# A tile loop whose output rows are normed and stored one tile earlier, with GpSimd's stores in front of its root

## The chip, the cores and the metric

The kernel runs on one core of a Trainium2 chip, as one launch. Every time here is device time of that core in microseconds (us). The kernel before was timed in three runs; one further execution was recorded by the hardware profiler, and all durations below are from that execution. The engines are TensorE (PE, with its weight loads as PEld), VectorE (DVE), ScalarE (ACT), GpSimd (POOL) and SyncE (SP, which here only starts DMA transfers).

## The reference, cut to what matters

The layer has three parts in a row, each followed by a residual sum and a layer norm. The first two are a selective state-space scan and a slot attention with three rounds of a gated cell. The change touches the third alone, a routed feed-forward layer with 8 experts over 64 x 128 tokens of 128 features:

```
x = x.reshape(-1, 128)                       # 8192 tokens
route = sigmoid(x @ Wr + br)
max_prob, max_ind = max(route), argmax(route)
for e in range(8):
    y = gelu(x @ W1[e]) @ W2[e]              # 128 -> 512 -> 128
    out += (max_ind == e) * y
out = out * max_prob
x = layernorm(x + out)                       # (v - mean) / sqrt(var + 1e-5) per token
```

## The kernel before, in words

The program has three stages, each a block of its own. The second leaves the tokens in a DRAM buffer, `sorted_x`, sorted by expert, with each token's probability and number beside it. The third stage, `expert_stage`, walks over that buffer in 39 tiles of 256 rows (`NJ`), each padded to belong to a single expert. It is the stage that the change touches.

Each engine has its own program, written out by hand as `tile(j, buf, turn, half)`, and `over_tiles` (L1470) unrolls it: tiles 0 to 8 one by one, then 30 tiles in a hardware loop of 6 at a time with `j` in a register, then a tail of a few tiles in which the late steps are finished. In its tile `j` an engine does steps that belong to tile `j` and to earlier tiles; `within(j, n)` asks whether tile `j - n` exists. Buffers are rings of six (`NBUF`), so `buf` is `j % 6`, and an even `buf` is an even `j`. The steps are these; "k" is the tile that a step works on.

- PE: in its tile j the transposes of tile j (L1657), the up matmuls of tile j-1 (L1668) and the down matmuls of tile j-2 (L1677). The down matmuls of tile k wait until `total` of tile k-2 has been written (`need(pe, summed, j - 1)`), since the two share a PSUM bank.
- ACT: in its tile j the two Gelus of tile j (L1560), and then the norm of tile j-5 (L1550): two activations, one for each half of 128 rows, that write `orow` from `total`, `shift` and `rstd`. For an even k it first waits until `shift` of the pair (k, k+1) is there; for each it waits until the store of tile k-6 has landed.
- DVE: in its tile j the copy of the transposed rows (L1607); in an odd tile j then `shift` of the pair that begins at j-5 (L1612), which waits for POOL's root; then for tile j-3 the target rows (L1617), `total` (L1619), and the moments (L1625, L1629); in an even tile j last `veps` of the pair that begins at j-4 (L1635).
- POOL: in an even tile j the root of the pair that begins at j-4 (L1526: `rstd` = `veps` to the power -0.5, for both tiles of the pair in one instruction, after a wait for `veps`); then the store of tile j-6 (L1531): a wait for the norm of that tile, and two indirect DMAs that scatter 128 rows each to `out_x`.
- SP: loads the rows and the two weight matrices of tile j, once `total` of tile j-6 has been written.

All of an engine's instructions run in the order in which they stand. POOL's root for a pair is therefore behind every store that is written before it, and DVE's `shift`, and with it all that follows on DVE, is behind the root.

Of the kernel before, what the change touches and what calls it, by code (L numbers as in the profile page):

```python
# [29 lines left out]
def need(eng, sem, value):  # L30

    if isinstance(value, int) and value <= 0:
        return
    eng.wait_ge(sem, value)


def hold(eng, sem, value, passed):


    eng.wait_ge(sem, value)  # L40
    eng.sem_inc(passed, 1)
# [1359 lines left out]
def expert_stage(nc, t, sb, psum, sem, ident, xs, scattered, base, base_start, e_index, out):  # L1401
# [7 lines left out]
    NJ = (NT + NE * (ROWS - 1)) // ROWS  # L1409
# [25 lines left out]
    ended = sb("ended", [P, NJ, NE])  # L1435
# [34 lines left out]
    def over_tiles(eng, tile, tail):  # L1470

        for j in range(PEEL):
            tile(j, j % NBUF, j // NBUF, j // 2)
        with eng.Fori(0, (NJ - PEEL) // NBUF) as i:
            for k in range(NBUF):
                j = PEEL + k
                tile(i * NBUF + j, j % NBUF, i + j // NBUF, i * (NBUF // 2) + j // 2)
        for j in range(NJ, NJ + tail):
            tile(j, j % NBUF, j // NBUF, j // 2)

    def earlier(buf, turn, back):

        return (buf - back) % NBUF, turn if buf >= back else turn - 1

    def within(j, back):

        return not isinstance(j, int) or back <= j < NJ + back

    def width(j):

        return min(2, NJ - j) if isinstance(j, int) else 2

    @blk.sync
    def _(sp):
        sp.wait_ge(step, N_STEPS)

        def load_rows(j, buf):
            r = sp.value_load(first_row[0:1, bass.ds(j, 1)], min_val=0, max_val=xs.shape[0] - ROWS)
            sp.dma_start(xrow[:, buf], xs[bass.ds(r, ROWS)].rearrange("(s p) d -> p s d", p=P)).then_inc(rows_in[buf], 16)

        def load_weights(j, buf):
            e = sp.value_load(expert[0:1, bass.ds(j, 1)], min_val=0, max_val=NE - 1)
            sp.dma_start(w1[:, buf], t["L0_ffn_W1"][bass.ds(e, 1)].rearrange("e d f -> d (e f)")).then_inc(weights_in[buf], 16)
            sp.dma_start(w2[:, buf], t["L0_ffn_W2"][bass.ds(e, 1)].rearrange("e (c p) d -> p (e c) d", p=P)).then_inc(weights_in[buf], 16)

        def tile(j, buf, turn, half):
            need(sp, summed, j - (NBUF - 1))
            load_rows(j, buf)
            if not isinstance(j, int) or j >= 1:
                load_weights(j, buf)  # L1510
        load_weights(0, 0)
        for lane in range(2):
            sp.wait_ge(scattered[lane], 16 * GB * NQ)
        over_tiles(sp, tile, 0)

    @blk.gpsimd
    def _(pool):
        pool.memset(m_half3[:], -0.5).then_inc(const3, 1)
        pool.memset(all_ones[:], 1.0).then_inc(const3, 1)
        pool.iota(j_index[:], pattern=[[1, NJ]], base=0, channel_multiplier=0, allow_small_or_imprecise_dtypes=True).then_inc(const3, 1)  # L1520
        pool.wait_ge(const3, 3)

        def root(j, buf, pair):
            pool.wait_ge(veps_done, pair + 1)
            w = width(j)
            pool.tensor_tensor(rstd3[:, buf:buf + w], veps3[:, buf:buf + w], m_half3[:, 0:w], ALU.pow).then_inc(rooted3, 1)  # L1526

        def store(j, buf):
            hold(pool, row_done, j + 1, passed3)
            for s in range(HALVES):  # L1530
                pool.indirect_dma_start(out_rows, bass.IndirectOffsetOnAxis(ap=target[:, buf, s:s + 1], axis=0), orow[:, buf, s], None,  # L1531
                                        bounds_check=NT - 1, oob_is_err=False).then_inc(out_stored[buf], 16)

        def tile(j, buf, turn, half):
            if buf % 2 == 0 and within(j, 4):
                root(j - 4, earlier(buf, turn, 4)[0], half - 2)
            if within(j, 6):
                store(j - 6, earlier(buf, turn, 6)[0])
        over_tiles(pool, tile, 6)
        for buf in range(NBUF):  # L1540
            pool.wait_ge(out_stored[buf], 16 * HALVES * len(range(buf, NJ, NBUF)))

    @blk.scalar
    def _(act):
        def normalised(j, buf, turn, pair):
            if buf % 2 == 0:
                act.wait_ge(shifted, pair + 1)
            need(act, out_stored[buf], turn * (16 * HALVES))
            for s in range(HALVES):
                ins = act.activation(orow[:, buf, s], total[:, buf, s], ACT.Identity, bias=shift3[:, buf, s:s + 1], scale=rstd3[:, buf, s:s + 1])  # L1550
            ins.then_inc(row_done, 1)

        def tile(j, buf, turn, half):
            par = buf % 2
            if within(j, 0):
                for m in range(2):
                    act.wait_ge(h_full, j * 2 + m + 1)
                    if m == 0:
                        need(act, y_full, j - 1)
                    act.activation(act_h[:, par, 2 * m:2 * m + 2].rearrange("p c r -> p (c r)"), ps_h[par][m][:], ACT.Gelu).then_inc(h_act, 1)  # L1560
            if within(j, 5):
                last, last_turn = earlier(buf, turn, 5)
                normalised(j - 5, last, last_turn, half - 2)
        over_tiles(act, tile, 5)

    @blk.vector
    def _(dve):
# [151 lines left out]
```

## Time and profile before

| | us |
|---|---|
| median of 3 runs | 1693.28 (1693.16 to 1693.36) |
| profiled execution, its own time | 1696.29 |
| span of its trace | 1694.1 |
| first instruction of `expert_stage` in the trace | 1511.86 |
| first transposes of the tile loop | 1521.44 |
| down matmuls of the last two tiles begin at | 1666.77 |
| last store is issued at | 1684.97 |

Over the whole span PE is busy 87%, DVE 74%, POOL 71% and ACT 65%. Times in the trace are counted from the start of the span. A row of the timeline is one instruction, or several of the same kind one behind the other ("x2"): its start, how long it took, the engine, the line, the operation with what it writes and reads, and in brackets how long the engine had been idle before it and what ended that. The tile to which a row belongs isn't written in it; it is found by counting from the start of the stage. The root at 1656.83 is that of tiles 32 and 33.

### The profile page before, as it was taken

The page shows a single profiled execution, that of the slowest core. Times are in us where ns is not written, and L with a number is a line of the kernel's source. Part 1 is how long each engine was busy: PE and PEld are TensorE (multiplying, and loading weights), DVE is VectorE, ACT ScalarE, POOL GpSimd, SP SyncE. Part 2 cuts the span into 40 slices and gives each one's busy share as a digit, 9 for nine tenths or more (in the row PEclk, how much of TensorE's full clock was granted, in tenths as well). Part 3 has the DMA queues.
Part 4 walks back from the last instruction along what each step waited for, and adds up shares of the span by engine and source line. Part 5 has one row for each costly group of instructions (what it writes and reads, how often), then busy time and mean ns, then how long its engine had stood idle before and what let it go on. Part 6 is the DMA issues. An engine that isn't in the chain of part 4 may idle for free. (4 is left out here: it accounts for less than half of the span.)

```text
span 1694.1 us, 21624 instructions
## 1 busy us (share of the span) xinstructions
PE 1470.6 (87%) x6178; PEld 880.2 (52%) x6178; DVE 1254.2 (74%) x2128; ACT 1099.0 (65%) x2149; POOL 1202.2 (71%) x863
## 2 busy tenths in 40 slices
PE   3888889888898889988885899999999999819994
PEld 1333334333343333433332677777777777619994
DVE  1999999999999999999991367666666666624452
ACT  3777787778877788777863566666566655404553
POOL 1899999999999999999993224555455445543665
PEclk8999999999999999999997999999999999859997
DMA  4454445444455455454431712122032000017771
GB/s 149 138 177 157 157 151 182 161 169 150 163 169 168 158 156 175 157 168 158 153 114 56 276 37 109 54 78 111 15 115 112 14 2 14 13 46 207 214 204 49
DMA packets 105846, 214.17 MB, mean 126 GB/s; under 512 B 12162, under 2 KB 56709, under 8 KB 105744
## 3 DMA queue, kind: packets, MB, share of 16 engines
q1 hardware_dynamic: 101200, 204.50, 36.4%
q0 software_dynamic: 4544, 8.47, 1.5%
q8 instruction: 45, 0.74, 0.2%
q14 instruction: 57, 0.47, 0.1%
HBM read 168.28 MB, written 45.56 MB: 126 GB/s over the span
## 5 line engine op out<-in xcount | busy, mean ns | idle before, releaser
L311 POOL TENSOR_TENSOR hc<-state,c_rows 128x1024 f32<-128x1024 f32 x256 | 598.4, 2359 | 41.4 <-DVE state L479 38.9
L479 DVE TENSOR_TENSOR_SCAN state<-ps_da,inp 128x512 f32<-128x512 f32 x512 | 594.4, 1211 | 25.9 <-ACT ps_da L391 25.9
L568 PE MATMUL ps_y<-hc,ident 128*128 128x512 f32 x1024 | 499.2, 633 | 71.0 <-POOL hc L311 71.0
L391 ACT ACTIVATE ps_da<-dt,a_neg 128x512 f32<-128x512 f32 x512 | 344.7, 687 | 124.3 <-DVE state L479 119.2
L568 PEld LDWEIGHTS ps_y<-hc,ident 128*128 128x128 f32 x1024 | 202.5, 203 | 344.6 <-issue 223.0
L468 DVE TENSOR_TENSOR inp<-dtx,ps_b 128x1024 f32<-128x1024 f32 x192 | 231.4, 1205 | 36.3 <-POOL dtx L286 24.0
L880 POOL TENSOR_TENSOR rs<-ms,m_half 128x4 f32<-128x4 f32 x48 | 49.5, 1032 | 246.1 <-DVE ms L1107 246.0
L298 POOL TENSOR_TENSOR inp<-dtx,b_rows 128x1024 f32<-128x1024 f32 x64 | 150.9, 2358 | 0.0
L521 PE MATMUL ps_misc<-x1T,w_conv 128*128 128x512 f32 (+3 forms) x256 | 119.4, 611 | 30.2 <-ACT x1T L337 22.0
L397 ACT COPY ps_b<-b_rows 128x512 f32<-128x512 f32 x192 | 111.3, 580 | 48.4 <-DVE inp L468 46.6
L1018 ACT ACTIVATE ex<-sc,nmx 77x128 f32<-77x128 f32 x192 | 74.9, 392 | 90.6 <-DVE nmx L1116 90.6
L1531 POOL DMA_INDIRECT out_x<-orow,target x78 | 77.0, 987 | 42.6 <-ACT orow L1550 22.2
L1112 DVE TENSOR_TENSOR sc<-sc,ps_s 77x512 f32<-77x512 f32 x48 | 32.8, 683 | 97.1 <-PE ps_s L1303 97.1
L1560 ACT ACTIVATE act_h<-ps_h 128x512 f32<-128x512 f32 x78 | 46.6, 598 | 82.6 <-PE ps_h L1668 79.5
L521 PEld LDWEIGHTS ps_misc<-x1T,w_conv 128*128 128x128 f32 x256 | 49.1, 197 | 97.1 <-issue 64.5
L919 POOL DMA_INDIRECT sorted_x<-row,dest x64 | 68.0, 1063 | 28.0 <-issue 14.6
L1677 PEld LDWEIGHTS ps_yy<-w,act_h 128*128 128x128 f32 x624 | 75.6, 192 | 2.0
L1668 PE MATMUL ps_h<-xcol,w 128*128 128x256 f32 x312 | 76.0, 388 | 0.0
L1677 PE MATMUL ps_yy<-w,act_h 128*128 128x128 f32 x624 | 75.8, 275 | 0.0
L1315 PEld LDWEIGHTS ps_s<-rse,ex 78*128 78x128 f32 x384 | 48.2, 192 | 33.0 <-DVE rse L1120 25.9
L1607 DVE COPY xcol<-ps_t 128x256 f32<-128x256 f32 x39 | 16.6, 425 | 65.0 <-PE ps_t L1657 65.0
L900 POOL TENSOR_SCALAR row<-tok,mv,rstd 128x128 f32<-128x128 f32 x64 | 58.5, 922 | 5.0 <-POOL rstd L896 5.0
(205 smaller groups left out, 2657.7 us busy)
## 6 DMA issues: line engine op xcount, KB each, us to landing
b_rows<-bc_rows SPq DMA_DIRECT2D x128, 512.0 KB, 4.7
c_rows<-bc_rows SPq DMA_DIRECT2D x128, 512.0 KB, 3.9
sorted_x<-pad_rows SPq DMA_DIRECT2D x8, 4160.0 KB, 14.0
w<-in_L_ffn_W SPq DMA_DIRECT2D x78, 256.0 KB
xrow<-sorted_x SPq DMA_DIRECT2D x39, 130.0 KB
x_tok<-in_x SPq DMA_DIRECT2D x16, 256.0 KB, 3.9
ctx<-in_ctx SPq DMA_DIRECT2D x16, 154.0 KB
out_x<-orow,target POOLq DMA_INDIRECT x78
```

What stands on the lines that cost most here:

```text
L298: pool.tensor_tensor(inp[:, n % RING], dtx[:, par], over_c(b_rows[:, slot, n % 2]), ALU.mult).then_inc(pool_fed, 1)
L311: pool.tensor_tensor(hc[:, n % RING], state[:, n % RING], over_c(c_rows[:, slot, n % 2]), ALU.mult).then_inc(hc_ready, 1)
L391: act.activation(ps_da[u % DA_RING][:], dt[:, par, c], ACT.Exp, scale=a_neg[:, c, n:n + 1]).then_inc(da_ready, 1)
L397: act.copy(ps_b[:], b_rows[:, slot, n % 2]).then_inc(b_copied, 1)
L468: dve.tensor_tensor(inp[:, n % RING], dtx[:, par], over_c(ps_b[:]), ALU.mult).then_inc(dve_fed, 1)
L479: dve.tensor_tensor_scan(state[:, n % RING, c], ps_da[u % DA_RING][:], inp[:, n % RING, c], 0.0, ALU.mult, ALU.add).then_inc(state_ready, 1)
L521: ins = pe.matmul(blocks[:, :, s:], w_conv[:, KW - 1 - s, c * P:(c + 1) * P], x_slot(g).rearrange("p (b l) -> p b l", l=P)[:, :, 0:P - s], ...
L568: ins = pe.matmul(ps_y[:, c], ident[:], hc[:, n % RING, c], start=False, stop=n == NS - 1)
L1018: act.activation(ex[lane][0:M, b * P:(b + 1) * P], sc[lane][:, b * P:(b + 1) * P], ACT.Exp, bias=nmx[lane][:, b:b + 1], accum_out=se[lane] ...
L1531: pool.indirect_dma_start(out_rows, bass.IndirectOffsetOnAxis(ap=target[:, buf, s:s + 1], axis=0), orow[:, buf, s], None, bounds_check=NT ...
L1668: ins = pe.matmul(ps_h[par][m][:, k * ROWS:(k + 1) * ROWS], w1[:, buf, c * P:(c + 1) * P], xcol[:, par], start=True, stop=True)
L1677: ins = pe.matmul(ps_yy[par][:, s * P:(s + 1) * P], act_h[:, par, c, s * P:(s + 1) * P], w2[:, buf, c], start=c == 0, stop=c == FC - 1)
```

## The change

ACT norms tile j-4 in its tile j in place of tile j-5, right behind the Gelus of tile j. POOL stores tile j-5 in its tile j in place of j-6. And in all tiles up to 38 POOL's store now stands in front of the root of its tile; in the tail (`ended`) the root stays in front. The tails of both engines are one tile shorter. DVE, PE and SP are as they were.

```
         def tile(j, buf, turn, half):
-            if buf % 2 == 0 and within(j, 4):
+            ended = isinstance(j, int) and j >= NJ
+            if ended and buf % 2 == 0 and within(j, 4):
                 root(j - 4, earlier(buf, turn, 4)[0], half - 2)
-            if within(j, 6):
-                store(j - 6, earlier(buf, turn, 6)[0])
-        over_tiles(pool, tile, 6)
+            if within(j, 5):
+                store(j - 5, earlier(buf, turn, 5)[0])
+            if not ended and buf % 2 == 0 and within(j, 4):
+                root(j - 4, earlier(buf, turn, 4)[0], half - 2)
+        over_tiles(pool, tile, 5)
...
-            if within(j, 5):
-                last, last_turn = earlier(buf, turn, 5)
-                normalised(j - 5, last, last_turn, half - 2)
-        over_tiles(act, tile, 5)
+            if within(j, 4):
+                last, last_turn = earlier(buf, turn, 4)
+                normalised(j - 4, last, last_turn, half - 2)
+        over_tiles(act, tile, 4)
```

Two places show what moves. The first is POOL at the head of its hardware loop, before the change; DMA rows are the stores, TENSOR_TENSOR the root, and the first two rows are the loop's head. Tile 9 stores tile 3, tile 10 has the root of (6, 7) and then stores tile 4, tile 11 stores tile 5.

```order
L1474 UNCONDITIONAL_BRANCH
L1474 ISA
L1531 DMA out_x<-orow,target 8192x128 [waits row_done]
L1531 DMA out_x<-orow,target 8192x128
L1524 ISA
L1526 TENSOR_TENSOR rstd<-veps,m_half 128x4 [waits veps_done]
L40 REGISTER_ALU
L1531 DMA out_x<-orow,target 8192x128 [waits row_done]
L1531 DMA out_x<-orow,target 8192x128
```

The same place after it: tile 9 stores tile 4, and tile 10 stores tile 5 and only then takes the root of (6, 7).

```order
L1474 UNCONDITIONAL_BRANCH
L1474 ISA
L1531 DMA out_x<-orow,target 8192x128 [waits row_done]
L1531 DMA out_x<-orow,target 8192x128
L40 REGISTER_ALU
L1531 DMA out_x<-orow,target 8192x128 [waits row_done]
L1531 DMA out_x<-orow,target 8192x128
L1524 ISA
L1526 TENSOR_TENSOR rstd<-veps,m_half 128x4 [waits veps_done]
```

The number of stores between two roots is the same, four DMAs; what is new is that the last two of them belong to the tile right in front of the pair whose root follows, where before they were those of two tiles further back.

The second place is ACT at the head of its loop, tile 9 before the change: the Gelus of tile 9 (L1560), then the norm of tile 4, which has to wait for `shift` of its pair.

```order
L34 REGISTER_ALU [waits h_full]
L1560 ACTIVATE act_h<-ps_h 128x512 [waits y_full]
L1557 REGISTER_ALU
L1560 ACTIVATE act_h<-ps_h 128x512 [waits h_full]
L1547 ISA
L34 REGISTER_ALU [waits shifted]
L1550 ACTIVATE orow<-total,shift,rstd 128x128 [waits out_stored4]
L1550 ACTIVATE orow<-total,shift,rstd 128x128
```

After it (three lines further down in the file) tile 9 norms tile 5, the second of its pair, without that wait, and the wait for `shift` stands in the even tiles.

```order
L34 REGISTER_ALU [waits h_full]
L1563 ACTIVATE act_h<-ps_h 128x512 [waits y_full]
L1560 REGISTER_ALU
L1563 ACTIVATE act_h<-ps_h 128x512 [waits h_full]
L34 REGISTER_ALU
L1553 ACTIVATE orow<-total,shift,rstd 128x128 [waits out_stored5]
L1553 ACTIVATE orow<-total,shift,rstd 128x128
```

So the wait for `shift` of a pair has moved from the ACT tile that is 5 behind to the one that is 4 behind, one tile closer to the root that it depends on.

## Rows read from the trace of the kernel before

**Rows 1.** The chain of waits that ended last: start us, us, what.

```profile
1683.39 0.30 issue
1683.69 0.97 POOL out_x L1531
1684.67 0.30 issue
1684.97 0.97 POOL out_x L1531
```

**Rows 2.** Busy time by stretch: the loop's steady part, and its end.

```profile
core 0: us, PE busy (x) PEld busy (x) DVE busy (x) ACT busy (x) POOL busy (x), PEclk, DMA share, GB/s
1550.00:1650.00 100.00, 100.00 (x698) 94.46 (x697) 50.57 (x243) 52.91 (x108) 67.45 (x68) 1.00 0.73 207
1670.00:1694.00 24.00, 0.51 (x5) 0.32 (x3) 2.32 (x14) 2.53 (x6) 12.79 (x14) 0.59 0.04 13
```

**Rows 3.** Timeline of PE: transposes of tiles 36 and 38, down matmuls of 36.

```profile
1653.85 0.38 PE L1657 MATMUL ps_t<-ident,xrow 128*128 128x128 f32 x2
...
1661.31 0.38 PE L1657 MATMUL ps_t<-ident,xrow 128*128 128x128 f32 x2
...
1663.26 1.95 PE L1677 MATMUL ps_yy<-w,act_h 128*128 128x128 f32 x16
```

**Rows 4.** Timeline of POOL from the root of pair 32 to that of 34.

```profile
1656.83 1.04 POOL L1526 TENSOR_TENSOR rstd<-veps,m_half 128x4 f32<-128x4 f32 x1
1658.24 1.03 POOL L1531 DMA_INDIRECT out_x<-orow,target  x1 [0.37 <-issue]
1659.58 0.97 POOL L1531 DMA_INDIRECT out_x<-orow,target  x1 [0.30 <-issue]
1661.96 0.98 POOL L1531 DMA_INDIRECT out_x<-orow,target  x1 [1.41 <-ACT orow L1550]
1663.24 0.97 POOL L1531 DMA_INDIRECT out_x<-orow,target  x1 [0.30 <-issue]
1664.40 1.04 POOL L1526 TENSOR_TENSOR rstd<-veps,m_half 128x4 f32<-128x4 f32 x1 [0.18 <-issue]
```

**Rows 5.** Timeline of ACT: norms of tiles 30 and 31, a Gelu between.

```profile
1656.49 0.87 ACT L1550 ACTIVATE orow<-total,shift,rstd 128x128 f32<-128x128 f32 x2
...
1659.73 0.60 ACT L1560 ACTIVATE act_h<-ps_h 128x512 f32<-128x512 f32 x1 [0.27 <-PE ps_h L1668]
1660.22 0.87 ACT L1550 ACTIVATE orow<-total,shift,rstd 128x128 f32<-128x128 f32 x2
```

**Rows 6.** Timeline of DVE: total of tile 33, veps and shift of pair 32, tile 34.

```profile
1654.77 0.61 DVE L1619 SCALAR_TENSOR_TENSOR total<-ps_yy,xrow 128x128 f32<-128x128 f32 x2
...
1656.55 0.19 DVE L1635 TENSOR_SCALAR veps<-mv 128x4 f32<-128x4 f32 x1
...
1658.43 0.15 DVE L1612 SCALAR_TENSOR_TENSOR shift<-mv,rstd 128x4 f32<-128x4 f32 x1
1658.50 0.16 DVE L1617 CAST target<-xrow 128x2 int32<-128x2 f32 x1
1658.57 0.61 DVE L1619 SCALAR_TENSOR_TENSOR total<-ps_yy,xrow 128x128 f32<-128x128 f32 x2
```

**Rows 7.** Timeline near the loop's start: last Gelus of tiles 4, 5; root of pair 2.

```profile
1540.31 0.60 ACT L1560 ACTIVATE act_h<-ps_h 128x512 f32<-128x512 f32 x1 [0.27 <-PE ps_h L1668]
...
1544.05 0.60 ACT L1560 ACTIVATE act_h<-ps_h 128x512 f32<-128x512 f32 x1 [0.27 <-PE ps_h L1668]
...
1544.75 1.01 POOL L1526 TENSOR_TENSOR rstd<-veps,m_half 128x4 f32<-128x4 f32 x1 [6.34 <-DVE veps L1635]
```

**Rows 8.** Timeline of POOL in the tail, root of pair 36 to root of 38.

```profile
1671.47 1.05 POOL L1526 TENSOR_TENSOR rstd<-veps,m_half 128x4 f32<-128x4 f32 x1
1672.71 1.03 POOL L1531 DMA_INDIRECT out_x<-orow,target  x1 [0.19 <-issue]
1674.05 0.97 POOL L1531 DMA_INDIRECT out_x<-orow,target  x1 [0.30 <-issue]
1675.32 0.97 POOL L1531 DMA_INDIRECT out_x<-orow,target  x1 [0.30 <-issue]
1676.60 0.97 POOL L1531 DMA_INDIRECT out_x<-orow,target  x1 [0.30 <-issue]
1677.59 0.74 POOL L1526 TENSOR_TENSOR rstd<-veps,m_half 128x2 f32<-128x2 f32 x1
```

**Rows 9.** Timeline in the tail: what the root of pair 36 releases.

```profile
1672.55 0.16 DVE L1612 SCALAR_TENSOR_TENSOR shift<-mv,rstd 128x4 f32<-128x4 f32 x1 [1.77 <-POOL rstd L1526]
...
1672.75 1.65 ACT L1550 ACTIVATE orow<-total,shift,rstd 128x128 f32<-128x128 f32 x4 [2.88 <-DVE shift L1612]
```

## The prediction

> **What bounds the kernel now.** I read the chain of waits first, since it says who holds the end. Its last pieces are stores on POOL with 0.30 between them [rows 1]: the program ends with POOL working off a queue of stores, and the last record ends at 1685.94 (1684.97 + 0.97). Next the busy time by stretch. In the steady part PE is busy 100 of 100 us, at its full granted clock, POOL 67; after 1670 PE has 0.5 us left and POOL still 12.8 [rows 2]. So there are two limits in a row: PE sets the pace of the loop, and after it a tail of POOL sets the end. Then the timelines, for the pace and for the room that each wait leaves. From the transposes of tile 36 to those of tile 38 it is 1661.31 - 1653.85 = 7.46 us: a pair of tiles costs 7.46, and PE never waits [rows 3]. The reader is to see in POOL's rows that, of the same 7.46, the root and four DMAs take most, that the second store of a pair begins only after 1.41 idle, released by ACT, and that the root of a pair comes before the stores [rows 4].
>
> **What moves, part by part.** No instruction is added or taken away, but for the tails, where ACT and POOL have the same work in a shorter frame. What counts is who waits for whom.
>
> ACT first. The norm of the even tile k now stands one tile earlier, behind the Gelus of tile k+4. By the rows that is behind a Gelu at 1659.73, where the norm of 31 starts at 1660.22 [rows 5]; `shift` of pair 32 is there at 1658.43 + 0.15 [rows 6]. This edit by itself would cost nothing: ACT would find its input ready, 1.6 us early. Its cover is that the root comes right behind `veps` (1656.55 + 0.19 against 1656.83 [rows 4, 6]).
>
> POOL takes that cover away. In an even tile its store now stands in front of the root, and that store waits for the norm of tile k-1. The norm of tile 31 would stand where that of 30 stands, 1656.49 to 1657.36 [rows 5]. From the end of a norm to the DMA that it releases there are 1661.96 - (1660.22 + 0.87) = 0.87 us [rows 4, 5], so the store would begin at 1658.23 and, as 0.97 + 0.30 + 0.97 = 2.24, end at 1660.47, and the root of pair 32 would start there, 3.6 us later than 1656.83. Queued behind the root are DVE's `shift`, and behind that target and `total` of tile 34, for which PE's down matmuls of tile 36 wait (1663.26 [rows 3]). From the start of a root to the end of that `total` it would be 1.04, then 0.03 to `shift` (1671.47 + 1.05 against 1672.55 [rows 8, 9]), then 0.07 + 0.07 and 0.61 [rows 6], together 1.82. `total` would be written at 1662.3, 1.0 before PE wants it. If that were all, PE would not feel it. A root can be 1663.26 - 1.82 - 1656.83 = 4.6 us late, less some 0.1 for the release, so 4.5.
>
> But there is now a ring. Root of pair k, `shift`, norm of k, store of k, store of k+1, root of pair k+2: each waits for the one before, on three engines, and none of it depends on PE. Its length, term by term:
> - root 1.04 [rows 4]; to `shift` 0.03; to the norm 1672.75 - 1672.55 = 0.20 [rows 9];
> - norm, both halves, 0.87 [rows 5]; from its end to the first DMA 0.87;
> - four DMAs of 0.97 with three gaps of 0.30, 4.78 [rows 8] (the second store's norm, behind two Gelus, I work out as done 0.7 us before POOL asks for it);
> - to the next root: 0.02 in the tail (1676.60 + 0.97 against 1677.59 [rows 8]), 0.19 in the loop (1663.24 + 0.97 against 1664.40 [rows 4]), where a wait for `veps` may be in it. I take 0.10.
>
> The sum is 7.89, against PE's 7.46. The ring is 0.43 longer, and the loop falls to its pace once the 4.5 us of room are used up. Before, the ring did not close: the root stood ahead of the stores and waited for `veps` alone.
>
> The bounds of it. Below: 0.02 for the last gap gives 7.81. Above: in the loop the counts that POOL waits for come out of registers. A store behind a root starts 0.37 after it in the loop and 0.19 in the tail [rows 4, 8]; no row shows two stores of neighbouring tiles back to back in the loop, so the middle gap may be 0.30 or 0.30 + 0.18. With that, and 0.19 in front of the root, it is 8.16. A gain from that gap is excluded, since the tail has no register work and still shows 0.30.
>
> Here a rule of the Trainium skill speaks against the change. A store beside DVE's work is in the rows already: the DMA at 1658.24 has `shift`, target and `total` of DVE inside it and takes 1.03, the last one of all, where DVE is long done, takes 0.97 [rows 1, 4, 6], so they cost each other 0.06 at most. The Trainium skill, page "SBUF — State Buffer", section "SBUF: two separate sides", says that DVE with two SBUF inputs and GpSimd exclude each other from a shared pair of ports for the whole instruction. By that rule `shift`, 0.15 once per pair, could stand in the ring once more, and 16 rounds of it would add 2.4 us; the trace does not bear that out for these shapes, and I leave it out of the sum.
>
> **The sum.** Start: the norm of tile 0 would run behind the last Gelu of tile 4 (0.49 behind its start, as 1660.22 - 1659.73), and that of tile 1 behind tile 5's: 1544.05 + 0.49 = 1544.54, done 1545.41 [rows 5, 7]. Store of tile 1 from 1546.28 to 1548.52, and the root of pair 2 at 1548.6, where it was at 1544.75 [rows 7]. That is 3.9 late already. From it to the root of pair 34 there are 16 rounds: 1548.62 + 16 x 7.89 = 1674.9. It was at 1664.40 [rows 4], so it is 10.5 late, and PE's end is 10.5 - 4.5 = 6.0 late.
>
> Tail, counted from the start R of the root of pair 34. Before: 1685.94 - 1664.40 = 21.5 us of POOL's records. After: norm of 34 done at R + 2.14, its store from 3.01 to 5.25; root of 36 (its `veps` is worked out at about 5.0: `total` of 36 at 1.8, then twice 1.36 from the end of `total` to the end of `veps` as 1654.77 + 0.61 against 1656.55 + 0.19 [rows 6], less the short wait between) from 5.27 to 6.31; store of 35 to 8.80; store of 36 to 11.34; root of 38, 0.74, to 12.10; stores of 37 and 38, with 0.19 and 0.30 in front, to 14.59 and 17.13. That is 4.4 us shorter: seven stores were queued behind this root (32 to 38), now it is five (34 to 38), 2 x 2.54 less, and a longer wait in front of the first. The end is 10.5 - 4.4 = 6.1 us later. With the ring at 7.81 it is 4.7, with 8.16 it is 10.4.
>
> For the profiled execution this makes 1696.29 + 6.1 = 1702.4. The median of the runs is 3.0 below that execution; nothing in the sum depends on that difference, so for the median 1693.28 + 6.1 = 1699.4.
>
> **Rivals.**
> - The ring is no longer than PE's pair. For it: several gaps are read from single rows, and of the 0.87 between norm and store a part might pass while POOL is still busy. Against it: 0.87 appears whenever POOL was already waiting, which it would be here every time. Then PE keeps 7.46, the root stays 3.6 late all along, inside its 4.5, and the end moves by 3.6 - 4.4 = -0.8: 1692.5, no change that can be told.
> - The change does what a shorter pipeline should do: rows leave a tile earlier, and the tail loses one store. A store is 2 x 1.27 = 2.5 us, and 1693.28 - 2.5 = 1690.8. For it: the end is POOL's queue of stores [rows 1]. Against it: a root that waits for a store. Even this is 0.15%; to be faster by more the loop's pace would have to fall, and PE is full.
> - More than the ring: a late `total` also holds back SP, whose loads for tile k+6 wait for that of tile k. Now 1661.31 + 3.73 - 1655.38 = 9.7 us lie between `total` of 33 and the place where the transposes of a tile 39 would stand [rows 3, 6]. In the ring, `total` of an even tile ends at R + 1.8, and PE comes to the transposes six tiles on at R + 1.9 + 1.8 + 3.7, only 5.6 after it. If rows then came 1 us late in each pair, 0.43 of that would fall into PE's idle time, and 16 x 0.57 = 9.1 would be added: 1708.5. Against it: DMA is 0.73 busy [rows 2], a slower loop asks less of it, and no transposes wait in the steady part.
>
> **Chances.** The ring 0.78; ring not binding 0.12; shorter tail alone 0.06; late loads on top 0.04. What this measurement can tell from no change is 0.2%, 3.4 us. The ring gives slower by more than that from its lower bound (4.7) up; a weak ring, say 7.65, would give 2.2 and count as no change. So slower 0.80, within 0.2% 0.16, faster by over 0.2% 0.04. Range: the ring's bounds are 1698.0 to 1703.7; I reach down to 1695.5 for a weak one and stop at 1703.5.
>
> **What would show it.** In POOL's timeline of the loop four DMAs stand in a row in front of each root, the first released by ACT's norm, and roots are 7.9 apart. PE's down matmuls of even tiles, from about tile 8 or 10 on, are preceded by 0.4 idle released by DVE's `total`, and none of odd tiles. The last matmul ends some 6 us later, while from there to the last store it is as before. The root of pair 2 is near 1548.6. I am wrong if roots stay 7.46 apart and PE has no idle time; wrong in size if the gaps between stores of neighbouring tiles in the loop are not 0.30.

## The result and the profile after

| | before | after |
|---|---|---|
| median of 7 runs | 1693.61 us (1693.16 to 1697.92) | 1701.79 us (1700.64 to 1704.81) |
| ratio to before, 95% interval | | 1.0048 (1.0039 to 1.0058) |
| profiled execution, its span | 1696.29, 1694.1 | 1704.81, 1702.1 |
| tile loop: first transposes to the end of the last store's record | 1521.44 to 1685.94, 164.5 | 1521.82 to 1693.93, 172.1 |

The changed kernel is slower by 8.2 us, and in the two profiled executions its tile loop is 7.6 us longer. Below I compare traces by that stretch, since the place where the loop begins moves by up to 5 us from one execution to another, whatever the kernel.

The chain of waits that ended last still consists of POOL's stores, as in [rows 1]; the columns are start us, us, what:

```profile
1692.65 0.30 issue
1692.95 0.98 POOL out_x L1531
```

Busy time by stretch shows that PE is no longer full in the loop's steady part (97.12 of 100 us); the columns are those of [rows 2]:

```profile
1550.00:1650.00 100.00, 97.12 (x658) 88.28 (x657) 49.91 (x233) 48.54 (x103) 62.40 (x63) 1.00 0.67 188
```

POOL's timeline of the changed kernel from one root to the next, in place of [rows 4]:

```profile
1596.83 1.07 POOL L1526 TENSOR_TENSOR rstd<-veps,m_half 128x4 f32<-128x4 f32 x1
1599.90 1.04 POOL L1531 DMA_INDIRECT out_x<-orow,target  x1 [1.99 <-ACT orow L1553]
1601.24 0.98 POOL L1531 DMA_INDIRECT out_x<-orow,target  x1 [0.30 <-issue]
1602.53 0.98 POOL L1531 DMA_INDIRECT out_x<-orow,target  x1 [0.30 <-issue]
1603.81 0.98 POOL L1531 DMA_INDIRECT out_x<-orow,target  x1 [0.30 <-issue]
1604.80 1.05 POOL L1526 TENSOR_TENSOR rstd<-veps,m_half 128x4 f32<-128x4 f32 x1
```

Four DMAs stand in a row in front of each root, and the idle time of 2 us is behind the root, released by ACT. Root to root it is 7.97 us, where it was 7.46. What the first of these roots releases, on DVE and ACT [rows 5, 6, 9]:

```profile
1597.94 0.16 DVE L1615 SCALAR_TENSOR_TENSOR shift<-mv,rstd 128x4 f32<-128x4 f32 x1 [3.45 <-POOL rstd L1526]
1598.02 0.17 DVE L1620 CAST target<-xrow 128x2 int32<-128x2 f32 x1
1598.10 0.60 DVE L1622 SCALAR_TENSOR_TENSOR total<-ps_yy,xrow 128x128 f32<-128x128 f32 x2
```

```profile
1598.14 0.88 ACT L1553 ACTIVATE orow<-total,shift,rstd 128x128 f32<-128x128 f32 x2 [2.72 <-DVE shift L1615]
1598.92 1.06 ACT L1563 ACTIVATE act_h<-ps_h 128x512 f32<-128x512 f32 x2
1599.88 0.87 ACT L1553 ACTIVATE orow<-total,shift,rstd 128x128 f32<-128x128 f32 x2
```

DVE stands idle for 3.45 us in front of `shift`, and the two Gelus of a tile are ready and queued behind the norm: they run one right behind the other, 1.06 us for both. PE's down matmuls [rows 3] in the changed kernel, of tiles 18, 19, 20 and 22:

```profile
1598.85 2.02 PE L1680 MATMUL ps_yy<-w,act_h 128*128 128x128 f32 x16 [0.34 <-DVE total L1622]
...
1602.66 1.95 PE L1680 MATMUL ps_yy<-w,act_h 128*128 128x128 f32 x16
...
1606.90 2.02 PE L1680 MATMUL ps_yy<-w,act_h 128*128 128x128 f32 x16 [0.35 <-DVE total L1622]
...
1614.75 2.02 PE L1680 MATMUL ps_yy<-w,act_h 128*128 128x128 f32 x16
```

Only even ones wait, for `total`. Two of three wait 0.33 to 0.36, and from one to the next it is up to 8.05; the third, here tile 22, comes 7.85 after the one before it, its idle time only 0.15. The mean is the 7.98 of the roots. Nothing of the loads is late: transposes waited for rows twice in the whole loop, both times at its start.

### The profile page after: what moved, and what is told of

The parts are those of the page before. It is cut to its first block and busy times, and to the rows that moved or that the text cites. A ratio compares the mean times of both kernels' runs of the same rounds, so it can differ in the third digit from the quotient of the medians.

```text
span 1702.1 us, 21628 instructions
## 1 busy us (share of the span) xinstructions
PE 1474.7 (87%) x6178; PEld 880.9 (52%) x6178; DVE 1256.3 (74%) x2128; ACT 1096.8 (64%) x2149; POOL 1202.2 (71%) x863
## 5 line engine op out<-in xcount | busy, mean ns | idle before, releaser
L1553 ACT ACTIVATE orow<-total,shift,rstd 128x128 f32<-128x128 f32 x78 | 33.8, 484 | 51.3 <-DVE shift L1615 51.3
```

## The experiments

"Stage" is the stretch from the first transposes to the end of the last store in the run's trace, less the 164.5 of before; "root to root" is the mean over the last twelve pairs of the loop, from the root of pair 10 to that of pair 34.

| run | ratio to before (95%) | stage | root to root |
|---|---|---|---|
| changed kernel | 1.0048 (1.0039 to 1.0058) | +7.6 | 7.98 |
| e1_norm_only | 0.9999 (0.9990 to 1.0008) | -0.7 | 7.45 |
| e2_no_swap | 0.9986 (0.9977 to 0.9995) | -2.6 | 7.45 |
| e3_swap_only | 1.0017 (1.0006 to 1.0028) | +0.7 | 7.46 |
| e4_store_swap | 1.0424 (1.0408 to 1.0440) | +69.2 | 11.81 |
| e5_late_shift | 1.0044 (1.0030 to 1.0058) | +7.7 | 7.98 |
| e6_middle | 0.9992 (0.9983 to 1.0001) | -1.1 | 7.46 |
| e7_before_more | 1.0038 (1.0024 to 1.0051) | +5.3 | 7.65 |
| e8_after_more | 1.0156 (1.0141 to 1.0172) | +25.8 | 8.93 |
| e9_two_of_three | 1.0006 (0.9993 to 1.0019) | -1.4 | 7.46 |
| e10_before_more_behind | 1.0011 (0.9995 to 1.0028) | +1.3 | 7.45 |

**Which part of the change costs.** The first three runs take the change apart; the fourth is the change without ACT's part.

e1_norm_only has ACT's part alone (the cut shows it against the kernel before):

```
-            if within(j, 5):
-                last, last_turn = earlier(buf, turn, 5)
-                normalised(j - 5, last, last_turn, half - 2)
-        over_tiles(act, tile, 5)
+            if within(j, 4):
+                last, last_turn = earlier(buf, turn, 4)
+                normalised(j - 4, last, last_turn, half - 2)
+        over_tiles(act, tile, 4)
```

> The kernel before with ACT's norm four tiles behind in place of five, POOL as it was (store six behind, root in front). Theory (a ring of root, shift, norm, two stores, next root that is longer than PE's pair): no store that stands in front of a root waits for the norm of the tile just ahead of it, so the ring is open; roots stay 7.46 us apart, PE has no idle time, and the time is that of the kernel before, 0 to -0.6 us. Rival (norming earlier makes ACT wait for shift and that holds up the Gelus, and through them PE): some of the 8 us lost by the changed kernel is there already, +2 us or more.

Measured: no change, 0.9999. In the list of who waited for whom (us in total, times, the longest), it is POOL's root that waits, for `veps`, 19 of 20 times:

```profile
POOL rstd L1526 <- DVE veps L1635: 53.9, 19, 25.3
```

The earlier norm costs nothing, and ACT waited for `shift` only in the tail.

e2_no_swap has ACT's part, and POOL's earlier store with the root always in front (POOL's tile against the kernel before):

```
             if buf % 2 == 0 and within(j, 4):
                 root(j - 4, earlier(buf, turn, 4)[0], half - 2)
-            if within(j, 6):
-                store(j - 6, earlier(buf, turn, 6)[0])
-        over_tiles(pool, tile, 6)
+            if within(j, 5):
+                store(j - 5, earlier(buf, turn, 5)[0])
+        over_tiles(pool, tile, 5)
```

> The changed kernel with POOL's root in front of its store in every tile (norm four behind, store five behind). Theory of the ring: root of pair k has only the stores up to tile k-2 in front of it, the ring is 7.98 less one store of two DMAs, about 5.4 us, under PE's 7.46; PE is not held up, roots are 7.46 apart, and the tail is one store (2 x 1.28 us) shorter: 2.5 us faster than the kernel before, 10 to 11 faster than the changed one. Rival (the earlier store is itself what costs, by its DMAs beside the loads or by landing waits): slower than before by 2 us or more with the root in front too.

Measured: 0.9986, 2.4 us faster than before (0.8 to 3.9), and the stage 2.6 shorter; PE is busy 100 of 100 us in the steady part. This is the version that beats both kernels. The rival, that the earlier store itself costs, is out.

e3_swap_only keeps 5 and 6 and moves POOL's store in front of its root in tiles up to 38, as the change does.

> The kernel before (norm five behind, store six behind) with POOL's store in front of its root in tiles up to 38. Theory of the ring: in front of the root of pair k stands the store of tile k-2, whose norm is long done; the ring has one store less and is open. Roots come later than before by about one store but stay 7.46 apart; the tail is up to 1.6 us longer. Rival (a root behind a store costs by itself, since DVE and PE wait behind the root, whatever the store waits for): most of the 8 us is there.

Measured: roots 7.46 apart, as the ring has it. By the ratio it is 2.9 us slower (1.0 to 4.7), by the stage 0.7; the expected 1.6 is between. PE waited for `total` once, in the tail:

```profile
PE ps_yy L1680 <- DVE total L1622: 1.2, 1, 1.2
```

One premise of the expectation is wrong. The norm of the store in front of the root is not long done: POOL waits 1.39 us for it in each pair.

```profile
1587.72 0.98 POOL L1531 DMA_INDIRECT out_x<-orow,target  x1 [1.39 <-ACT orow L1553]
1589.00 0.98 POOL L1531 DMA_INDIRECT out_x<-orow,target  x1 [0.30 <-issue]
1589.99 1.06 POOL L1526 TENSOR_TENSOR rstd<-veps,m_half 128x4 f32<-128x4 f32 x1
```

But that norm, five tiles behind, had its `shift` some 2 us before it started (1583.61 + 0.16 against 1585.98): ACT waited for `shift` only in the tail, and its norms follow the Gelus at PE's pace. So a root behind a store costs nothing in the loop as long as the norm of that store does not have to wait for the root before.

e4_store_swap is e3_swap_only with `store(j - 5, ...)`, the norm left five behind.

> The kernel before (norm five behind) with POOL's store five behind and in front of its root: the changed kernel without the earlier norm. Theory of the ring: the root of pair k now waits for the store of tile k-1, that for its norm, which stands behind the Gelus of tile k+4, and these behind PE, which waits for the total behind the root. The ring then goes through PE: 0.2 to the last Gelu, 0.49, norm 0.87, 0.88 to the store, 2.25 for its two DMAs, root 1.06, 0.03, total 0.77, 0.06 to the down matmuls of k+4, 1.78, transposes 0.22, up matmuls 1.73, together 10.3 us for a pair: some 50 us slower than before, and with more PE idle time of 2.9 us for each pair. Rival (a fixed cost of a root behind a store, or of the store one tile earlier): near the changed kernel, +8 us, at most +15.

Measured: 1.0424, 72 us slower; the theory said 50 and the rival at most 15. PE's down matmuls of an even and of the next odd tile in its timeline:

```profile
1610.92 3.75 PE L1680 MATMUL ps_yy<-w,act_h 128*128 128x128 f32 x16 [2.80 <-DVE total L1622]
...
1617.66 1.95 PE L1680 MATMUL ps_yy<-w,act_h 128*128 128x128 f32 x16
```

The idle time is 2.8 to 2.9 in all sixteen rounds, as expected. Seven of them take 10.5 to 10.6, close to the 10.3 worked out for the ring through PE, and the sixteen down matmuls behind the idle time take 2.02. The other nine take 11.9 to 13.6, and in them the matmuls behind the idle time are slow, 2.5 to 3.75 for the same sixteen. Why these nine and not the others stays open. The granted clock of the steady part says it too, 0.90 where it was 1.00 (column eight of busy time by stretch):

```profile
1550.00:1650.00 100.00, 74.40 (x440) 67.11 (x439) 33.53 (x155) 34.30 (x68) 43.69 (x44) 0.90 0.44 125
```

The mechanism held; of the 22 us on top some 17 are the nine longer rounds (111.7 against 9 x 10.54), with their slow matmuls, which I had not priced. So the mechanism is confirmed by the seven undisturbed rounds, not by the total.

**Ring, or total behind the root.** e5_late_shift takes `total` out from behind the root; the cut is from DVE's tile, against the changed kernel:

```
-            if buf % 2 and within(j, 5):
-                shift(j - 5, earlier(buf, turn, 5)[0], half - 2)
             if within(j, 3):
                 last, last_turn = earlier(buf, turn, 3)
                 gated(j - 3, last, last_turn)
                 moments(j - 3, last)
+            if buf % 2 and within(j, 5):
+                shift(j - 5, earlier(buf, turn, 5)[0], half - 2)
```

> The changed kernel with DVE's shift moved behind total and the moments of its tile, so that total no longer stands behind the root. Theory of the ring: the ring of root, shift, norm, two stores, root stays closed at 7.9 to 8.0 us; PE is then held through ACT (Gelus behind norms) in place of DVE, and the end, which POOL's roots and stores set, is as in the changed kernel: +6.5 to +8.5 us against before. Rival (what costs is DVE's total behind a late root, 0.35 us of PE idle time per pair, and no ring): that idle time is gone, roots are 7.46 apart, and the kernel is at the time of the one with no swap, -2.5 us, or near before.

Measured: 1.0044, as the changed kernel, roots 7.98 apart. `total` no longer holds PE, and the time is the same; the ring is the cause, and `total` only the way by which PE felt it. One detail was wrong: PE is now held not by the Gelus but by the column copy, which stands behind `shift` on DVE:

```profile
1615.62 1.99 PE L1671 MATMUL ps_h<-xcol,w 128*128 128x256 f32 x8 [0.33 <-DVE xcol L1610]
```

**Shortening the ring.** e6_middle is e2_no_swap with the root of even tiles between the two DMAs of the store (`store` got a third argument, the half).

> Norm four behind, store five behind, and the root between the two DMAs of the store in even tiles, the tail included. Theory of the ring: one DMA (1.28 us) leaves the part of the ring that is in front of the next root: 7.98 - 1.28 = 6.7 us, under 7.46; the ring is open, PE has no idle time, though root and total are about 2.5 us later than with no swap. -2.0 us against before. Rival (a root behind a store of the same tile costs in proportion): half of the changed kernel's loss, about +3 us.

Measured: 0.9992 (-1.4 us, interval -2.9 to +0.2), stage -1.1, roots 7.46 apart. With one DMA less in front of the root the roots keep PE's pace: the ring is open. The rival's +3 is outside the interval.

**Lengthening it.** e7_before_more and e8_after_more add the same line to `root` of the kernel before and of the changed one; `spare3` is a new scratch tile.

```
         def root(j, buf, pair):
+            pool.tensor_tensor(spare3[:, buf:buf + 2], all_ones[:, 0:4].rearrange("p (a s) -> p a s", a=2), m_half3[:], ALU.pow)
             pool.wait_ge(veps_done, pair + 1)
```

> The kernel before with one more power of the root's size on POOL, on constants into a scratch tile, in front of each root's wait for veps (1.05 us, 20 of them). Control for the next one. Theory of the ring: POOL has 7.46 - 6.6 = 0.9 us to spare for each pair and no ring; in the tail the added ones of the last pairs count: +2 us. Rival (POOL's load as such is the limit): +10 us or more.

> The changed kernel with the same added power in front of each root's wait. It stands in the ring, behind the stores. Theory of the ring: each of 16 rounds becomes 1.05 us longer, 9.0 us, and the kernel 17 to 19 us slower than the changed one, +25 to +27 against before, more if the granted clock falls with PE's idle time of 1.5 us per pair, as it fell in the run with norm five and store five behind. Rival (no ring, the changed kernel's loss a fixed one per root): as for the kernel before, 2 us on top of the changed kernel, +10.

Measured: e8 is 26.4 us slower than before (1.0156), 18 more than the changed kernel, its roots 8.93 apart, 0.96 more. That is the theory's number. POOL's root with the added power in front, and the PE wait that answers to it:

```profile
1611.25 1.06 POOL L1525 TENSOR_TENSOR spare<-all_ones,m_half 128x4 f32<-128x4 f32 x1
1612.28 1.01 POOL L1528 TENSOR_TENSOR rstd<-veps,m_half 128x4 f32<-128x4 f32 x1
```

```profile
1614.34 2.02 PE L1682 MATMUL ps_yy<-w,act_h 128*128 128x128 f32 x16 [1.31 <-DVE total L1624]
```

The control e7 missed: 6.4 us slower (1.0038), not 2, with roots uneven (7.1 to 8.6) and on average 7.65 apart in the last twelve pairs, 7.75 over all sixteen. It stays well below e8's step of 18, so the place in the ring is what makes the power dear, but it is not the free one I took it for.

e10_before_more_behind has the same added line behind the root's own power, so that POOL's load is the same and the root stays where it was.

> The kernel before with the added power behind each root and in front of the stores. With it in front of the root, the control cost 6.4 us in place of 2, and its trace shows DVE's column copy held until the added power had ended. If POOL's load as such costs (7.27 us of work in 7.46, with nothing left for an uneven pace), this one costs the same, +5 to +7. If it is that the added power stands between the last store and the root, and so delays root and shift, this one, which leaves the root where it was, costs only the tail, +2.

Measured: 1.0011 (-0.8 to +4.7 us), stage +1.3, roots 7.45 apart: the place matters, not the load. It also takes back what its expectation says of e7's copies: here DVE's column copy runs beside the added power, in its usual 0.42:

```profile
1610.43 1.00 POOL L1528 TENSOR_TENSOR spare<-all_ones,m_half 128x4 f32<-128x4 f32 x1
```

```profile
1610.67 0.42 DVE L1609 COPY xcol<-ps_t 128x256 f32<-128x256 f32 x1 [1.35 <-PE ps_t L1659]
```

So such a power does not by itself hold a copy up. In e7 all the same, in nine of the fifteen pairs between 1550 and 1665 the column copy starts within 0.2 us after the added power has ended, and in none do the two overlap:

```profile
1591.54 1.06 POOL L1525 TENSOR_TENSOR spare<-all_ones,m_half 128x4 f32<-128x4 f32 x1
```

```profile
1592.61 0.42 DVE L1609 COPY xcol<-ps_t 128x256 f32<-128x256 f32 x1 [2.35 <-PE ps_h L1670]
```

ACT's Gelus are late too there, by up to 3 us after the up matmuls that they wait for, and they start while the power still runs (1592.30); in e8 the same is seen (3.03 in front of the Gelu at 1612.11). What holds these instructions stays open, and with it the cause of e7's 4 us beyond the forecast. The Trainium skill, page "SBUF — State Buffer", section "SBUF: two separate sides", has a GpSimd operation exclude a DVE operation in a two-port mode, and one that reads SBUF exclude a DVE operation with two SBUF inputs, each for a whole instruction. `shift` has two SBUF inputs, and in e10 it runs inside the added power in its usual 0.15, so the trace does not show that exclusion for it:

```profile
1611.01 0.15 DVE L1614 SCALAR_TENSOR_TENSOR shift<-mv,rstd 128x4 f32<-128x4 f32 x1
```

**Fixed cost or ring.** e9_two_of_three is the changed kernel with the root in front in one of three even tiles (against the changed kernel).

```
+            behind = not ended and buf in (0, 2)
+            if not behind and buf % 2 == 0 and within(j, 4):
                 root(j - 4, earlier(buf, turn, 4)[0], half - 2)
             if within(j, 5):
                 store(j - 5, earlier(buf, turn, 5)[0])
+            if behind and buf % 2 == 0 and within(j, 4):
                 root(j - 4, earlier(buf, turn, 4)[0], half - 2)
```

> Norm four behind, store five behind, POOL's store in front of its root in two of three even tiles (those whose buffer is 0 or 2), the root in front in the third (buffer 4). Theory of the ring: two rounds of it are 2 x 7.98 or somewhat more, and the third, with the root in front of one store, is more than 2 us shorter and is set by veps, that is by PE; the three together need no more than 3 x 7.46 = 22.4, so the lag is worked off in each turn of the loop and only the last turn's remains: 0 us against before (between -2.5 and +1.5). Rival (the loss is a fixed one for each swapped root): two thirds of the changed kernel's 10.7 us against the one with no swap, that is +4.6 against before.

Measured: 1.0006 (-1.2 to +3.2 us), stage -1.4; the rival's +4.6 is outside. The roots in its timeline:

```profile
1558.23 1.04 POOL L1526 TENSOR_TENSOR rstd<-veps,m_half 128x4 f32<-128x4 f32 x1
...
1567.18 1.07 POOL L1526 TENSOR_TENSOR rstd<-veps,m_half 128x4 f32<-128x4 f32 x1
...
1575.13 1.06 POOL L1526 TENSOR_TENSOR rstd<-veps,m_half 128x4 f32<-128x4 f32 x1
...
1580.59 1.04 POOL L1526 TENSOR_TENSOR rstd<-veps,m_half 128x4 f32<-128x4 f32 x1
```

They are 8.95, 7.95 and 5.46 apart, 22.36 for three, which is PE's 3 x 7.46 within rounding. Between these roots there are six, four and two DMAs, since the root in front stands one store earlier. One open round in three works off what the two others lose. A fixed price for a root behind a store would not do that.

## Why the prediction was right, and where it was off

The forecast was 6.1 us slower; measured are 8.2, 7.6 of them in the tile loop.

- *The ring is longer than PE's pair.* Right: e2, e6 and e9 open it and are not slower than before, e5 leaves it closed and is as slow as the change, e8 lengthens it and pays for each round. Rows of after and of e5 show it on every engine.
- *Its length, 7.89.* Too small: it is 7.98 on average. By the round shown above (7.97) the terms are root 1.07, 0.04, 0.20, norm 0.88, 0.88 to the first DMA, 4.89 for the four, 0.01 to the next root. The four DMAs were priced at 4.78: behind a root the first takes 1.04 even after 2 us of idle time, where I took 0.97, and the others take 0.98. The prediction put such a 1.03 down to DVE's work beside the store. That reading was wrong: the DMA behind the last root, at 1689.04, takes 1.04 too, though DVE's last instruction ends 0.01 after its start. Those beside DVE's work but behind another store take 0.98. The last gap, where I chose 0.10, is 0.01. One round in three takes 8.01 to 8.05. The register work that I kept as an upper bound for the gap between stores of neighbouring tiles does not show: 0.30.
- *The start.* Root of pair 2 at 1548.97, 27.15 after the first transposes against 23.31 before: 3.84 late, 3.87 predicted.
- *Sixteen rounds.* 1676.59 - 1548.97 = 127.6 against 126.2; this 1.4 us is nearly the whole of what the sum lacked. The root of pair 34 is 11.8 late, not 10.5.
- *The tail.* From that root to the last record 17.3 us, 17.1 predicted, 21.5 before. Stage +7.6; the sum with the measured ring is 11.8 - 4.2 = 7.6. The other 0.6 of the 8.2 between the medians is less than the executions scatter.
- *Room of 4.5 us, and PE's idle time.* The down matmuls of tile 10 are the first to be late, by 0.24 (predicted: from tile 8 or 10 on), and from tile 12 on two of three even tiles wait 0.33 to 0.36 (predicted 0.4) and the third 0.13 to 0.15. The idle time is not all that PE loses: between tiles 18 and 20 the pair is 0.59 longer, of which 0.35 is idle, 0.16 is that the up matmuls in front run out before it (1.89 in place of 1.73 to the next start), and 0.08 is the start behind it (1.86 in place of 1.78). The down matmuls of tile 36 are 7.0 late, for a root that is 11.4 late: 4.4 of room.
- *PE's end 6.0 late.* Wrong: it is 11.2. The room of 4.5 is that of the full loop. The last down matmuls of before had no transposes and up matmuls in front of them and started at 1668.55 (1666.77 + 1.78), only 2.3 after what their `total` allowed (1664.40 + 1.82); in the changed kernel they waited for 2.41 us and then ran at 3.51 in place of 1.95. The end did not hang on it, since POOL's chain from the root of 34 was summed by itself. For the same reason the sign named for it failed: from PE's end to the last record it is 11.8 us, where before it was 15.4; the prediction had named it unchanged.

```profile
1678.59 3.51 PE L1680 MATMUL ps_yy<-w,act_h 128*128 128x128 f32 x16 [2.41 <-DVE total L1622]
```

- *Rivals.* The shorter tail is real, and e2 shows what it is worth alone, the 2.5 predicted for it. Late row loads did not occur. `shift` does not stand in the ring twice: its start is 0.04 behind the root's end.

## What to carry to other kernels

When an engine's queue is reordered, follow the waits from the moved instruction through the other engines until they come back to it. If they do, add up that ring and compare it with the pace of the bound engine: it costs nothing up to there, and its excess in every round beyond. A spare round now and then, or one instruction less in front of the wait, was enough to open it here. Room that an even loop gives to a late result is gone at its ends, where the engine that waits has less to do in between.

## What the runs showed of the hardware that was not expected

- An indirect store on POOL took 1.03 to 1.06 us behind a tensor operation, also with 2 us of idle time between (changed kernel), and 0.95 to 0.99 behind another store, also with 2.8 to 5.9 us of idle time between (e4).
- Idle time of PE of 0.34 and of 1.3 us in each pair left the granted clock of the steady part at 1.00 (changed kernel, e8). With 2.8 to 2.9 us per pair (e4) it was 0.90: in nine of sixteen rounds the matmuls behind the idle time were slow, at worst 3.75 us for sixteen, with a granted clock of 0.50 from 1611.0 to 1614.5, which is the lower of the two levels, 1.2 GHz; in seven rounds, behind the same idle time, they took 2.02. In the tail of the changed kernel 2.41 us of idle time were followed by a granted clock of 0.54 (1678.6 to 1682.0).
- The DMA record behind another store was mostly 0.97 in some of these kernels (before, e1, e7, e8, e10) and mostly 0.98 in the others; what sets it I did not find.
